# Reordered loads, split key and value weights, and zero products on TensorE at the start of a gated cross-attention and mixture-of-experts kernel

## The chip, the cores and the metric

One NeuronCore of a Trainium2 chip runs the whole program. The metric is the device time in microseconds (us), from a median of three runs. The profile is one execution of the same program; its times are microseconds from the start of its span.

## The reference

```python
x = x + tanh(g_xattn) * xattn(layernorm(x), ctx)   # x: 8 batches x 56 tokens x 256
x = x + tanh(g_ffn)   * moe(layernorm(x))          # 16 experts, 2 per token, one shared

def xattn(x, cond, ...):                           # cond: 8 x 1500 x 256
    q = qdq(x) @ qdq(wq).T + bq                    # qdq: round to int8 and back, by row
    k, v = split(cond @ wkv.T + bkv)               # 256 columns of keys, 256 of values
    attn = softmax(q @ k.T / 4)                    # 16 heads of 16
    return qdq(attn @ v) @ qdq(wp).T + bp
```

Four inputs of this matter here: the tokens x (448 KB), the key and value weights wkv (512 KB), the query weights wq (256 KB) and the context of the first batch, which is loaded in three chunks of 500 context rows (500 KB each).

## The kernel before

Keys and values are computed in 16-bit halves: a high half is a rounded copy, a low half is what the copy lost, and a product is three partial products (high by high, high by low, low by high), each in two parts of 128 for the contraction. So one group of keys (`project_keys(n, u)`) is 6 matmuls of 500 columns, and one group of values (`project_values(n, v)`) is 12 matmuls of 256 columns, all recorded under line 1035 (`split3`). Each batch has 6 groups of each kind. ScalarE (ACT) makes the high halves (`context_hi`, L479; weights L472), VectorE (DVE) the low halves of the first two batches (`context_lo`, L715; weights L721).

There is no planner: each engine has its instructions in an order written out by hand, and waits for counters (semaphores). The order of each engine before the first attention slot, which is what the change touches:

- **SP**, the load queue: tokens (L291), key and value weights in one transfer (L293), context chunk 0, query weights in two transfers (L298), chunks 1 and 2; then the chunks of batch 1, each after the low half of the chunk before it, and the copies that stack the keys (`stack_keys`, L312).
- **ACT**: three small transfers (columns of biases L468, broadcast rows L469, router weights L470), high half of the key and value weights (L472), scaling of the key bias (L565), high halves of chunk 0, tanh of the gate (L567), chunk 1, then keys and values out of the accumulators as TensorE finishes them (`keys_hi` L486, `evacuate_values` L493), between them the query path (L574, L577, L580).
- **DVE**: layer-norm statistics of the tokens (L697 to L703), low half of the weights, low half of chunk 0, `quantise_first` (L708, L678 to L692: the first 112 tokens), low half of chunk 1, low half of the first keys (`keys_lo`, L743), scales (L737), quantisation of the query weights (L678 to L692), low half of chunk 2, second keys, the query product (L749) and its halves, then the other 336 tokens (`quantise_rest`), further keys and the second query product.
- **POOL**: constants (L365 to L385), one power for the layer norm (L390), then more constants, `zero16` among them (L402, 112 x 512 zeros in 16 bits, read only much later).
- **PE** (TensorE): waits for the constants and for the low halves, then keys 0, values 0 and 1, turns the quantised tokens (L1199, L1206), keys 1, turns the query weights (L1223), values 2, first query product (L1213), values 3, keys 2, values 4 and 5, keys 3 and 4, turns the other tokens, keys 5, second query product, and the attention slots (`pe_slot`).

After the prologue come 64 attention slots (8 batches of 8 pairs of heads), in which the keys and values of the next batch are fitted between scores (L1078), turned scores (L1101) and outputs (L1112), then the output projection, the router and the experts.

Of the kernel before, what the change touches and what calls it, by code (L numbers as in the profile page):

```python
# [17 lines left out]
ALU = mybir.AluOpType  # L18
ACT = mybir.ActivationFunctionType
AX = mybir.AxisListType  # L20

B, S, D = 8, 56, 256
# [5 lines left out]
TP, TT = 112, 4  # L28
# [15 lines left out]
NCONST = 24  # L44
NSMALL = 3 * 16
# [64 lines left out]
def program(nc, x, ctx, cols, rows, gate, wq, wkv, wp, W13, W2, out):  # L110
    stack = ExitStack()
    with stack:
# [132 lines left out]
        names = """consts var_ready rstd_ready sp_ready x_loaded wq_loaded wp_loaded wkv_loaded small_loaded xq_ready xr_ready wqq_ready wpq_ready  # L245
# [44 lines left out]
        def _(sp):  # L290
            sp.dma_start(x_in[:], x.rearrange("b s d -> (b s) d").rearrange("(t p) d -> p t d", p=TP)).then_inc(s["x_loaded"], 16)  # L291

            sp.dma_start(wkv_in, wkv).then_inc(s["wkv_loaded"], 16)  # L293
            for c in range(CH):
                sp.dma_start(c_in[:, :, c * CW:(c + 1) * CW], ctx_v[0, :, :, c * CW:(c + 1) * CW]).then_inc(ctx_in[c], 16)
                if c == 0:
                    for k in range(NH):
                        sp.dma_start(wq_in[:, k, :], permuted(wq[k * 128:(k + 1) * 128, :])).then_inc(s["wq_loaded"], 16)  # L298
# [63 lines left out]
        def _(gp):  # L362
            c = Steps(gp, s["consts"])
            for t, v in ((mhalf, -0.5), (unmagic, -MAGIC), (ident, 0.0), (ident16, 0.0), (ones, 1.0), (ones16, 1.0), (before16, 1.0), (hm2, 1.0)):
                c.did(gp.memset(t[:], v))  # L365
# [36 lines left out]
            c.did(gp.memset(zero16[:], 0.0))  # L402
# [28 lines left out]
            gp.wait_ge(s["act_pre"], 3)  # L431
# [33 lines left out]
        def _(act):  # L465
            ap = Steps(act, s["act_pre"])

            act.dma_start(col_in[:], cols).then_inc(s["small_loaded"], 16)  # L468
            act.dma_start(row_in[:], rows.partition_broadcast(TP), allow_slow_non_contiguous=True).then_inc(s["small_loaded"], 16)  # L469
            act.dma_start(gateT[:], gate).then_inc(s["small_loaded"], 16)  # L470
            act.wait_ge(s["wkv_loaded"], 16)
            ap.did(act.activation(wkvT[:, 0], wkv_in, ACT.Copy, scale=WS))  # L472
# [90 lines left out]

            act.wait_ge(s["small_loaded"], NSMALL)
            ap.did(act.activation(bk_c, bk_c, ACT.Copy, scale=WS))  # L565
            context_hi(0, 0)
            ap.did(act.activation(tg[:, 0:1], gx[:, 0:1], ACT.Tanh))  # L567
            context_hi(0, 1)
            act.wait_ge(s["act_pre"], 2)
            keys_hi(0, 0)  # L570
# [4 lines left out]
            evacuate_values(0, 1)  # L575
            act.wait_ge(s["pe_pre"], 2)
            ap.did(act.activation(sx_row[:, 0:TP], PS[:, 1, 0:TP], ACT.Copy))  # L577
            keys_hi(0, 1)
            act.wait_ge(s["pe_pre"], 3)
            ap.did(act.activation(wqT[:], bank16(7)[:, 0:NH * D].rearrange("p (h t) -> p h t", h=NH), ACT.Copy))  # L580
            evacuate_values(0, 2)
# [90 lines left out]
        def _(dve):  # L672
# [44 lines left out]

            dve.wait_ge(s["x_loaded"], 16)
            statistics(x_in, range(TT))
            dve.wait_ge(s["act_pre"], 1)  # L720
            dve.scalar_tensor_tensor(wkvT[:, 1], wkv_in, WS, wkvT[:, 0], ALU.mult, ALU.subtract).then_inc(s["dve_pre"], 1)  # L721
            context_lo(0, 0)
# [16 lines left out]

            def keys_lo(n, u):  # L740
                oh, c = divmod(u, CH)
                need(dve, "kh_done", n * 6 + u + 1)
                dve.scalar_tensor_tensor(KN[:, oh, c, 1, :], PS[:, BANK["K", n, u], 0:CW], bk_c[:, oh:oh + 1],  # L743
                                         KN[:, oh, c, 0, :], ALU.add, ALU.subtract).then_inc(s["kl_done"], 1)
# [19 lines left out]
            context_lo(0, 1)  # L764
            keys_lo(0, 0)
# [6 lines left out]
            dve.wait_ge(s["small_loaded"], NSMALL)  # L772
# [90 lines left out]
            for k, part in enumerate(groups):  # L863
                n = part.stop - part.start
                out_ps = PS[0:TP, out_bank[part.start]:out_bank[part.start] + n, :].rearrange("p t (h j) -> p t h j", j=PW)
                dve.wait_ge(s["pe_post"], k + 1)
                d.did(dve.tensor_scalar(rd[:, part, :], out_ps[:, :, :, DH], WS, None, ALU.mult))
                d.settle()
                d.did(dve.reciprocal(rd[:, part, :], rd[:, part, :]))
                d.settle()  # L870
                dve.tensor_tensor(xn[:, part, :].rearrange("p t (h j) -> p t h j", h=H), out_ps[:, :, :, 0:DH],
                                  rd[:, part, :].unsqueeze(3).to_broadcast([TP, n, H, DH]), ALU.mult).then_inc(s["out_read"], 1)
                dve.wait_ge(s["out_read"], k + 1)
                d.settle()
                d.did(dve.tensor_tensor(xn[:, part, :], xn[:, part, :], bv_r.unsqueeze(1).to_broadcast([TP, n, D]), ALU.add))
                quantise(xn[:, part, :], n, am[0:TP], so[:, part], xq16[:, part, :]).then_inc(s["oq_done"], 1)
# [151 lines left out]
        def _(pe):  # L1028
# [8 lines left out]

            pe.wait_ge(s["consts"], EARLY)
# [150 lines left out]
            project_keys(0, 0)  # L1189
            project_values(0, 0)  # L1190
            project_values(0, 1)

# [25 lines left out]
            project_keys(0, 1)  # L1218
# [218 lines left out]
```

## Time and profile before

| | us |
|---|---|
| device time, median of 3 runs | 407.97 (407.75, 407.97, 412.41) |
| span of the profiled execution | 405.0 |
| PE busy in it | 358.6 |
| DVE busy in it | 303.5 |
| ACT busy in it | 250.9 |
| POOL busy in it | 124.1 |

Of the profiled execution only its span is given, from the first to the last instruction; its device time is not among the numbers shown. The span is 2.97 us under the median of the runs. In the profile, a row of the timeline gives start, duration, engine, line of the code, operation, what is written from what, and the count of instructions merged; the brackets give how long the engine stood idle before it and what ended that.

### The profile page before, as it was taken

How to read it: one execution, taken by the hardware profiler on the slowest of the kernel's cores; microseconds unless marked ns; L12 is line 12 of the kernel's file. 1: busy time of each engine (PE TensorE's matmuls, PEld its weight loads, DVE VectorE, ACT ScalarE, POOL GpSimd, SP SyncE). 2: the span in 40 equal slices, each digit the busy share in tenths (PEclk: the TensorE clock that was granted, in tenths of full speed). 3: DMA queues.
4: the chain of work that ended last, by engine and by line, in shares of the span. 5: the costliest groups of instructions: out<-in, count | busy, mean ns of one | idle time of the engine just before them, and what ended most of it. 6: DMA issues, size and time to landing. Idle time of an engine off the chain costs nothing.

```text
span 405.0 us, 14019 instructions
## 1 busy us (share of the span) xinstructions
PE 358.6 (89%) x5793; PEld 269.3 (67%) x5793; DVE 303.5 (75%) x656; ACT 250.9 (62%) x412; POOL 124.1 (31%) x116
## 2 busy tenths in 40 slices
PE   0896899999998998998999999998864699999993
PEld 0663468668677766855866776786643587888882
DVE  3888886775776676586577668668896877999993
ACT  3476477777686676776768666567721535666761
POOL 6151462132022122222203300001101054787870
PEclk9999699999999999999999999999985858999998
DMA  7869965565294186166336208544000009635001
GB/s 253 196 157 197 241 146 134 87 159 136 58 171 115 53 152 182 54 106 175 103 61 125 54 14 142 129 137 141 3 2 2 1 1 306 191 116 163 2 0 45
DMA packets 34512, 45.65 MB, mean 113 GB/s; under 512 B 3995, under 2 KB 30299, under 8 KB 34323
## 3 DMA queue, kind: packets, MB, share of 16 engines
q1 hardware_dynamic: 33395, 43.74, 44.5%
q0 software_dynamic: 640, 0.78, 0.9%
q8 instruction: 46, 0.75, 0.8%
q10 hardware_dynamic: 416, 0.26, 0.3%
q14 instruction: 15, 0.12, 0.1%
HBM read 25.08 MB, written 0.47 MB: 63 GB/s over the span
## 4 chain that ended last, share of the span: by engine, by line
PE 76%; DVE 13%; issue 5%; ACT 2%; POOL 2%; DMA 1%; DVEq 0%; ACTq 0%; POOLq 0%
PE PS L1035 35%; PE PS L1101 9%; PE PS L1078 8%; PE PS L1112 7%; PE PS L1363 4%; PE PS L1322 3%; DVE mx L794 2%; PE PS L1088 2%; PE PS L1346 2%; PE PS L1312 1%; DMA x_in<-x 1%; DVE KN L743 1%; PE PS L1279 1%; DVE st L697 1%; DVE mtop L798 1%
## 5 line engine op out<-in xcount | busy, mean ns | idle before, releaser
L794 DVE TENSOR_REDUCE mx<-PS 112x1 f32<-112x500 f32 (+1 forms) x128 | 114.3, 933 | 52.8 <-PE PS L1078 52.7
L501 ACT ACTIVATE PT_all<-PS 128x1344 f32<-128x1344 f32 x64 | 82.6, 1290 | 10.1 <-PE PS L1101 9.9
L1035 PE MATMUL PS<-cT,wkvT 128*128 128x500 f16 x288 | 71.5, 385 | 18.0 <-POOL slot_of L404 11.2
L1035 PE MATMUL PS<-wkvT,cT 128*125 128x256 f16 x576 | 73.2, 279 | 0.0
L1035 PEld LDWEIGHTS PS<-wkvT,cT 128*125 128x125 f16 x576 | 65.3, 139 | 5.3 <-issue 0.5
L395 POOL TENSOR_TENSOR cT<-c_in,cT 128x1000 f16<-128x1000 f32 x18 | 37.5, 2082 | 86.9 <-ACT cT L479 86.9
L1035 PEld LDWEIGHTS PS<-cT,wkvT 128*128 128x128 f16 x288 | 27.5, 99 | 50.8 <-POOL slot_of L404 11.2
L486 ACT ACTIVATE KN<-PS,col_in 128x500 f16<-128x500 f32 x48 | 32.5, 677 | 40.6 <-PE PS L1035 40.6
L1078 PE MATMUL PS<-arena,QC 96*112 96x500 f16 x192 | 52.4, 380 | 3.1 <-issue 2.8
L1101 PE MATMUL PS<-QC,arena 98*128 98x112 f16 x768 | 49.2, 214 | 3.0 <-ACT QC L521 2.9
L493 ACT ACTIVATE V<-PS 125x512 f32<-125x512 f32 x48 | 28.7, 598 | 30.6 <-PE PS L1035 30.6
L1101 PEld LDWEIGHTS PS<-QC,arena 98*128 98x128 f16 x768 | 41.6, 99 | 8.3 <-ACT QC L521 3.1
L743 DVE SCALAR_TENSOR_TENSOR KN<-PS,col_in,KN 128x500 f16<-128x500 f32 x48 | 35.2, 736 | 12.8 <-ACT KN L486 12.0
L1112 PE MATMUL PS<-PT_all,V 125*17 125x56 f32 x2592 | 37.8, 213 | 0.1
L449 POOL TENSOR_TENSOR arena<-arena 88x512 f16<-88x512 f32 x17 | 24.8, 1458 | 31.2 <-ACT arena L527 31.1
L1035 PE MATMUL PS<-arena 88*128 88x256 f16 (+2 forms) x216 | 33.3, 306 | 0.8 <-ACT arena L635 0.7
L1112 PEld LDWEIGHTS PS<-PT_all,V 125*17 125x17 f32 x2592 | 33.3, 98 | 0.2 <-issue 0.2
L419 POOL TENSOR_TENSOR QC<-q,par 96x448 f16<-96x448 f16 x16 | 15.0, 943 | 57.1 <-PE PS L1101 55.3
L1035 PEld LDWEIGHTS PS<-arena 88*128 88x128 f16 (+2 forms) x216 | 22.5, 106 | 9.0 <-issue 1.2
L1078 PEld LDWEIGHTS PS<-arena,QC 96*112 96x112 f16 x192 | 20.3, 132 | 9.8 <-issue 3.8
L479 ACT ACTIVATE cT<-c_in 128x1000 f16<-128x1000 f32 x24 | 24.9, 1036 | 2.0 <-DMA c_in<-ctx 1.6
L1088 PEld LDWEIGHTS PS<-ident,nm 112*2 112x2 f16 x64 | 5.1, 79 | 21.9 <-issue 17.3
(207 smaller groups left out, 463.8 us busy)
## 6 DMA issues: line engine op xcount, KB each, us to landing
arena<-KN SPq DMA_DIRECT2D x144, 125.0 KB, 3.6
c_in<-ctx SPq DMA_DIRECT2D x24, 500.0 KB, 4.5
cT<-W SPq DMA_DIRECT2D x11, 352.0 KB
c_in<-W SPq DMA_DIRECT2D x6, 352.0 KB
cT<-W SPq DMA_DIRECT2D x11, 176.0 KB
arena<-place_far SPq DMA_DIRECT2D x1, 1568.0 KB, 10.0
c_in<-W SPq DMA_DIRECT2D x6, 176.0 KB
PT_all<-L_xattn_wkv SPq DMA_DIRECT2D x1, 512.0 KB, 6.1
```

What stands on the lines that cost most here:

```text
L395: gp.tensor_tensor(cT[:, n % 2, 1, :, c * CW:(c + 1) * CW], c_in[:, :, c * CW:(c + 1) * CW], cT[:, n % 2, 0, :, c * CW:(c + 1) * CW], ALU. ...
L449: gp.tensor_tensor(w2T[j % 2][:, 1], w2_s, w2T[j % 2][:, 0], ALU.subtract).then_inc(s["w2l_done"], 1)
L479: act.activation(cT[:, n % 2, 0, :, c * CW:(c + 1) * CW], c_in[:, :, c * CW:(c + 1) * CW], ACT.Copy).then_inc(s["th_done"], 1)
L486: act.activation(KN[:, oh, c, 0, :], PS[:, BANK["K", n, u], 0:CW], ACT.Identity, bias=bk_c[:, oh:oh + 1]).then_inc(s["kh_done"], 1)
L493: act.activation(V[:, n % 2, 2 * v:2 * v + 2, :, 0:DH], PS[0:KP, BANK["V", n, v], :].rearrange("p (t h j) -> p t h j", t=2, h=H), ACT.Copy ...
L501: act.activation(PT_all[:, u % 4, :].rearrange("p (c k) -> p c k", c=CH), PS[:, 3:6, 0:4 * TP], ACT.Exp, scale=SCORE).then_inc(s["exp_done ...
L743: dve.scalar_tensor_tensor(KN[:, oh, c, 1, :], PS[:, BANK["K", n, u], 0:CW], bk_c[:, oh:oh + 1], KN[:, oh, c, 0, :], ALU.add, ALU.subtract ...
L794: dve.tensor_reduce(mx[:, u % 2, k:k + 1], PS[0:TP, k:1 + k * (CH - 1), 0:CW], AX.XY, ALU.max).then_inc(s["red_done"], 1)
L1035: ins = mm(out_, w(a, h), x_(b, h), start=first and k == 0, stop=last and k == len(todo) - 1)
L1078: mm(PS[0:TP, c, 0:CW], QC[0:QR, b % 2, i * TP:(i + 1) * TP], KS[0:QR, b % 2, i, c * CW:(c + 1) * CW], start=True, stop=True).then_inc(s[" ...
L1101: last = mm(PS[:, 3 + t // 4, (t % 4) * TP:(t % 4 + 1) * TP], KS[0:QR + 2, b % 2, i, t * KP:t * KP + 128], QC[0:QR + 2, b % 2, i * TP:(i + ...
L1112: last = mm(PS[32 * j:32 * j + VW, bank, 0:S], V[:, b % 2, t, 4 * hg + j, :], PT[:, (2 * g + j // 2) % 4, t * TP + (j % 2) * S:t * TP + (j ...
```

## The change

The loads go out in the order key weights, chunk 0, value weights, tokens, chunk 1, query weights, chunk 2. The key and value weights come in two transfers with a counter each, and their high and low halves are made apart. ACT issues the broadcast rows and the router weights after the conversion of the key weights; the columns have a counter of their own. `zero16` becomes POOL's first constant, and TensorE multiplies it 24 times into a bank that nothing reads before its next use. On ACT the high half of chunk 1 moves behind the first `keys_hi`; on DVE the statistics move behind the low halves of weights and chunk 0, and `quantise_first` behind the low halves of chunk 1 and of the first keys. On PE keys 1 and values 2 move ahead of the turned tokens, values 3 ahead of the first query product.

```diff
 SP
-  x_in, wkv_in (all), context chunk 0, wq x2, chunk 1, chunk 2
+            sp.dma_start(wkv_in[:, :, 0:D], wkv[:, :, 0:D]).then_inc(s["wk_loaded"], 16)
             for c in range(CH):
                 sp.dma_start(c_in[...c...], ctx_v[0, ...c...]).then_inc(ctx_in[c], 16)
                 if c == 0:
+                    sp.dma_start(wkv_in[:, :, D:2 * D], wkv[:, :, D:2 * D]).then_inc(s["wv_loaded"], 16)
+                    sp.dma_start(x_in[:], ...).then_inc(s["x_loaded"], 16)
+                if c == 1:
                     for k in range(NH): sp.dma_start(wq_in[:, k, :], ...)
 POOL
+            gp.memset(zero16[:], 0.0).then_inc(s["zeros_ready"], 1)
...
-            c.did(gp.memset(zero16[:], 0.0))
 ACT
-            act.wait_ge(s["wkv_loaded"], 16)
-            ap.did(act.activation(wkvT[:, 0], wkv_in, ACT.Copy, scale=WS))
+            act.wait_ge(s["wk_loaded"], 16)
+            ap.did(act.activation(wkvT[:, 0, :, 0:D], wkv_in[:, :, 0:D], ACT.Copy, scale=WS))
...
+            act.dma_start(row_in[:], rows.partition_broadcast(TP), ...)
+            act.dma_start(gateT[:], gate)
             context_hi(0, 0)
+            act.wait_ge(s["wv_loaded"], 16)
+            ap.did(act.activation(wkvT[:, 0, :, D:2 * D], wkv_in[:, :, D:2 * D], ACT.Copy, scale=WS))
+            act.wait_ge(s["col_loaded"], 16)
+            ap.did(act.activation(bk_c, bk_c, ACT.Copy, scale=WS))
+            act.wait_ge(s["act_pre"], 3)
+            keys_hi(0, 0)
+            context_hi(0, 1)
+            act.wait_ge(s["small_loaded"], NSMALL)
+            act.activation(tg[:, 0:1], gx[:, 0:1], ACT.Tanh).then_inc(s["tg_ready"], 1)
             evacuate_values(0, 0)
+            evacuate_values(0, 1)
             context_hi(0, 2)
+            keys_hi(0, 1)
 DVE
+            for k in range(2):
+                part = slice(k * D, (k + 1) * D)
+                dve.wait_ge(s["act_pre"], k + 1)
+                dve.scalar_tensor_tensor(wkvT[:, 1, :, part], wkv_in[:, :, part], WS, wkvT[:, 0, :, part], ...)
+                if k == 0:
+                    context_lo(0, 0)
+            dve.wait_ge(s["x_loaded"], 16)
+            statistics(x_in, range(TT))
+            context_lo(0, 1)
+            keys_lo(0, 0)
             quantise_first()
-            context_lo(0, 1)
-            keys_lo(0, 0)
 PE
+            pe.wait_ge(s["zeros_ready"], 1)
+            for k in range(WARM):            # WARM = 24
+                mm(PS[0:TP, 7, :], zero16[:, 0:TP], zero16[:], start=True, stop=True)
             pe.wait_ge(s["consts"], EARLY)
...
             pe.wait_ge(s["dve_pre"], 1)
             project_keys(0, 0)
+            pe.wait_ge(s["dve_pre"], 2)
             project_values(0, 0)
             project_values(0, 1)
+            project_keys(0, 1)
+            project_values(0, 2)
             turn_tokens([0], 1)
             turn_scales([0], 1)
-            project_keys(0, 1)
             pe.wait_ge(s["wqq_ready"], 1)
...
-            project_values(0, 2)
+            project_values(0, 3)
             pe.wait_ge(s["act_pre"], 6)
             project_queries(...)
-            project_values(0, 3)
```

## Rows read from the trace of the kernel before

**Rows 1.** The page: busy time of each engine; granted TensorE clock in 40 slices.
```profile
PE 358.6 (89%) x5793; PEld 269.3 (67%) x5793; DVE 303.5 (75%) x656; ACT 250.9 (62%) x412; POOL 124.1 (31%) x116
...
PEclk9999699999999999999999999999985858999998
```
**Rows 2.** The page: shares of the chain of work that ended last, by engine.
```profile
PE 76%; DVE 13%; issue 5%; ACT 2%; POOL 2%; DMA 1%; DVEq 0%; ACTq 0%; POOLq 0%
```
**Rows 3.** Timeline, loads landed and converted: start, duration, instruction, [idle before, ended by].
```profile
4.98 1.41 DVE L697 BATCH_NORM_STATS2 st<-x_in 112x6 f32<-112x256 f32 x4 [4.98 <-DMA x_in<-x]
...
7.16 1.04 POOL L390 TENSOR_TENSOR rstd<-var,mhalf 112x4 f32<-112x4 f32 x1 [1.84 <-DVE var L703]
7.36 1.06 ACT L472 ACTIVATE wkvT<-PT_all 128x1024 f16<-128x1024 f32 x1 [3.81 <-DMA PT_all<-L_xattn_wkv]
...
8.45 1.23 DVE L721 SCALAR_TENSOR_TENSOR wkvT<-PT_all,wkvT 128x1024 f16<-128x1024 f32 x1 [1.45 <-ACT wkvT L472]
8.78 1.04 ACT L479 ACTIVATE cT<-c_in 128x1000 f16<-128x1000 f32 x1 [0.27 <-DMA c_in<-ctx]
...
9.85 1.20 DVE L715 TENSOR_TENSOR cT<-c_in,cT 128x1000 f16<-128x1000 f32 x1 [0.18 <-ACT cT L479]
```
**Rows 4.** Timeline, TensorE's first groups and two of the same kind later.
```profile
11.20 2.66 PE L1035 MATMUL PS<-cT,wkvT 128*128 128x500 f16 x6 [11.20 <-POOL slot_of L404]
...
13.65 4.50 PE L1035 MATMUL PS<-wkvT,cT 128*125 128x256 f16 x24
...
23.95 2.78 PE L1035 MATMUL PS<-wkvT,cT 128*125 128x256 f16 x24
...
31.08 1.43 PE L1035 MATMUL PS<-cT,wkvT 128*128 128x500 f16 x6
```
**Rows 5.** Timeline, VectorE from the first tokens to the second query product.
```profile
10.97 0.52 DVE L708 TENSOR_SCALAR xn<-x_in,mv,rstd 112x256 f32<-112x256 f32 x1
...
13.08 0.29 DVE L692 TENSOR_SCALAR xq<-xn 112x256 f16<-112x256 f32 x1
...
14.67 0.74 DVE L743 SCALAR_TENSOR_TENSOR KN<-PS,col_in,KN 128x500 f16<-128x500 f32 x1 [0.19 <-ACT KN L486]
...
17.74 0.43 DVE L692 TENSOR_SCALAR wq<-PT_all 128x512 f16<-128x512 f32 x1
...
20.54 0.74 DVE L743 SCALAR_TENSOR_TENSOR KN<-PS,col_in,KN 128x500 f16<-128x500 f32 x1 [1.26 <-ACT KN L486]
...
21.66 0.58 DVE L749 SCALAR_TENSOR_TENSOR qT<-PS,swq,sx_row 128x112 f32<-128x112 f32 x2 [0.38 <-PE PS L1213]
...
24.86 0.74 DVE L743 SCALAR_TENSOR_TENSOR KN<-PS,col_in,KN 128x500 f16<-128x500 f32 x1 [0.41 <-ACT KN L486]
...
33.19 1.04 DVE L749 SCALAR_TENSOR_TENSOR qT<-PS,swq,sx_row 128x336 f32<-128x336 f32 x2 [0.97 <-PE PS L1213]
```
**Rows 6.** Timeline, ScalarE: high half of chunk 1, and the first keys.
```profile
11.23 1.04 ACT L479 ACTIVATE cT<-c_in 128x1000 f16<-128x1000 f32 x1 [1.31 <-DMA c_in<-ctx]
...
13.96 0.68 ACT L486 ACTIVATE KN<-PS,col_in 128x500 f16<-128x500 f32 x1 [1.70 <-PE PS L1035]
```
**Rows 7.** Timeline: the zeros, and one of ACT's transfers being issued.
```profile
1.25 0.51 ACTq L469 DMA_DIRECT2D row_in<-rows  x1
...
10.26 0.63 POOL L402 MEMSET zero<- 112x512 f16 x1
```
**Rows 8.** DMA view of 0 to 40 us: GB/s in each microsecond; one load's size and landing.
```profile
GB/s 0 20 119 371 327 274 253 369 379 395 404 185 118 122 172 148 300 306 191 83 92 352 297 162 36 59 191 208 71 14 237 134 174 135 142 142 156 156 299 411
...
PT_all<-L_xattn_wkv SPq DMA_DIRECT2D x1, 512.0 KB, 6.1
```
**Rows 9.** Later: TensorE's longest early gap, then busy times and granted clock (PEclk).
```profile
40.84 2.50 PE L1035 MATMUL PS<-cT,wkvT 128*128 128x500 f16 x6 [2.35 <-DVE cT L715]
...
40.00:45.00 5.00, 3.20 (x14) 1.33 (x14) 3.86 (x8) 1.57 (x3) 0.00 (x0) 0.61 1.04 276
45.00:50.00 5.00, 5.00 (x30) 3.02 (x28) 4.12 (x6) 2.63 (x4) 4.01 (x6) 0.71 1.13 206
```

More of the change, by code:

```diff
@@ L43 @@
 EARLY = 16
-NCONST = 24
-NSMALL = 3 * 16
+NCONST = 23
+NSMALL = 2 * 16
+WARM = 24
 ROWS = 2 * D + E + 2
@@ L466, in _ @@
             ap = Steps(act, s["act_pre"])
-            act.dma_start(col_in[:], cols).then_inc(s["small_loaded"], 16)
-            act.dma_start(row_in[:], rows.partition_broadcast(TP), allow_slow_non_contiguous=True).then_inc(s["small_loaded"], 16)
-            act.dma_start(gateT[:], gate).then_inc(s["small_loaded"], 16)
-            act.wait_ge(s["wkv_loaded"], 16)
-            ap.did(act.activation(wkvT[:, 0], wkv_in, ACT.Copy, scale=WS))
+            act.dma_start(col_in[:], cols).then_inc(s["col_loaded"], 16)
+            act.wait_ge(s["wk_loaded"], 16)
+            ap.did(act.activation(wkvT[:, 0, :, 0:D], wkv_in[:, :, 0:D], ACT.Copy, scale=WS))
             def context_hi(n, c):
@@ L562, in act_slot @@
                     w13_hi(0)
-            act.wait_ge(s["small_loaded"], NSMALL)
[L565 to L570, printed above, removed]
+            act.dma_start(row_in[:], rows.partition_broadcast(TP), allow_slow_non_contiguous=True).then_inc(s["small_loaded"], 16)
+            act.dma_start(gateT[:], gate).then_inc(s["small_loaded"], 16)
+            context_hi(0, 0)
+            act.wait_ge(s["wv_loaded"], 16)
[5 more added lines that the diff above has]
+            context_hi(0, 1)
+            act.wait_ge(s["small_loaded"], NSMALL)
+            act.activation(tg[:, 0:1], gx[:, 0:1], ACT.Tanh).then_inc(s["tg_ready"], 1)
             evacuate_values(0, 0)
+            evacuate_values(0, 1)
             context_hi(0, 2)
+            keys_hi(0, 1)
             act.wait_ge(s["pe_pre"], 1)
             ap.did(act.activation(xqT[:, :, 0:TP], bank16(7)[:, 0:NH * TP].rearrange("p (h t) -> p h t", h=NH), ACT.Copy))
-            evacuate_values(0, 1)
             act.wait_ge(s["pe_pre"], 2)
             ap.did(act.activation(sx_row[:, 0:TP], PS[:, 1, 0:TP], ACT.Copy))
-            keys_hi(0, 1)
+            evacuate_values(0, 2)
             act.wait_ge(s["pe_pre"], 3)
             ap.did(act.activation(wqT[:], bank16(7)[:, 0:NH * D].rearrange("p (h t) -> p h t", h=NH), ACT.Copy))
-            evacuate_values(0, 2)
             context_hi(1, 0)
@@ L716, in context_lo, with keys_lo @@
                                   cT[:, n % 2, 0, :, c * CW:(c + 1) * CW], ALU.subtract).then_inc(s["tl0_done"], 1)
+            def keys_lo(n, u):
+                oh, c = divmod(u, CH)
+                need(dve, "kh_done", n * 6 + u + 1)
+                dve.scalar_tensor_tensor(KN[:, oh, c, 1, :], PS[:, BANK["K", n, u], 0:CW], bk_c[:, oh:oh + 1],
+                                         KN[:, oh, c, 0, :], ALU.add, ALU.subtract).then_inc(s["kl_done"], 1)
+            for k in range(2):
+                part = slice(k * D, (k + 1) * D)
+                dve.wait_ge(s["act_pre"], k + 1)
+                dve.scalar_tensor_tensor(wkvT[:, 1, :, part], wkv_in[:, :, part], WS, wkvT[:, 0, :, part],
+                                         ALU.mult, ALU.subtract).then_inc(s["dve_pre"], 1)
+                if k == 0:
+                    context_lo(0, 0)
             dve.wait_ge(s["x_loaded"], 16)
             statistics(x_in, range(TT))
-            dve.wait_ge(s["act_pre"], 1)
-            dve.scalar_tensor_tensor(wkvT[:, 1], wkv_in, WS, wkvT[:, 0], ALU.mult, ALU.subtract).then_inc(s["dve_pre"], 1)
-            context_lo(0, 0)
+            context_lo(0, 1)
+            keys_lo(0, 0)
             def quantise_first():
```

15 lines of the change are left out of this document (5 added, 10 removed).

## The prediction

> **What bounds the kernel now.** I read the busy shares first: PE is busy for 89% of the span, DVE for 75% [rows 1]. The chain of waits agrees: 76% of the span is PE work, 13% DVE [rows 2]. The change touches none of that bulk. It can only move the moment at which the attention slots begin, and every microsecond gained there is one at the end, since the slots follow at PE's pace. So the timeline of the first 35 us decides, with one question: which engine sets that moment?
>
> There, PE stands idle until 11.20 us. It waits for the low half of chunk 0, which DVE ends at 9.85 + 1.20 = 11.05; the profile names POOL's L404, but that is only the last event by time, and PE waits for nothing POOL does then [rows 3, 4]. Before it the loads land one behind the other: tokens at 4.96, weights at 7.35, chunk 0 at about 8.75 [rows 3]. PE's first groups take long besides: six 500-column matmuls start 2.45 us before the next group, 0.408 each, and later ones take 1.43 for six with their tail. The 24 value matmuls take 4.50 against 2.78 [rows 4]. So the first matmuls are at the 1.2 GHz level, the later at 2.4.
>
> But PE catches up, and what then holds the slots is DVE. From 8.45 on it is almost never idle: its waits before the second query product are 0.19, 1.26, 0.38, 0.41 and 0.97 [rows 5]. That product starts at 33.19 and ends at 34.23; the first scores wait for it. A change that starts PE sooner is worth only what it takes out of those waits, or what it moves DVE's work forward.
>
> **Loads.** I add up the GB/s row: 0.51 MB are moved by 4 us, 0.84 by 5, 1.11 by 6, 1.36 by 7, 1.73 by 8, 2.11 by 9, 2.51 by 10 [rows 8]. The combined weights land at 1.25 + 6.1 = 7.35, when 1.49 MB are through; ahead of their end stand 0.98 MB of SP loads and 0.25 of ACT's. So a load lands when the curve passes its bytes plus some 0.27. Key weights (0.26 MB): about 4.1. Chunk 0 (0.77): 5.8, or 6.7 if ACT's 0.25 MB, issued by then, get their share in front; I take 6.0. Value weights: 7.5. Tokens: 8.7. Chunk 1: 10.1. Query weights 10.8.
>
> **ACT and DVE up to chunk 0.** Half of the 1.06 conversion, with its fixed part, is about 0.6 [rows 3]: ACT has the key weights by 4.75, DVE by 5.4. ACT then issues two transfers, 0.51 for such a one [rows 7], until 5.8, hidden by the wait for chunk 0. Chunk 0 is high at 7.1 and low at 8.3. That is 2.75 us sooner than 11.05. The halves cost one more fixed part on each engine, about 0.1, in waits.
>
> **Zero products.** POOL's zeros take 0.63 [rows 7] from 0.8, so PE starts at 1.45; POOL's other constants slip by as much and nobody waits for them. 24 products of 512 columns take 0.418 each at the lower clock (0.408 x 512/500) and 0.215 at the higher (0.21 for 500, from 1.43 less a tail of 0.17). The bounds are 1.45 + 5.2 = 6.6, all at the higher, and 1.45 + 10.0 = 11.5, all at the lower. How long was the clock low before? With x us at 0.209 per value matmul and the rest at 0.108, 24 = x/0.209 + (4.33 - x)/0.108 gives x = 3.6: low from 11.20 to 17.25, 6.0 us [rows 4]. I take that row: 14.4 products at 0.418, 9.6 at 0.215, and the end at **9.55**. That is 1.25 after the data at 8.3: the zero products, not the loads, now start the first keys, still 1.65 sooner than 11.20.
>
> **Where the gain goes.** Keys 0 are ready at 9.55 + 1.43 = 11.0, against 13.86. ACT now has the high half of chunk 1 behind `keys_hi` of that group: 0.68 from 11.05, then 1.04 [rows 6], so chunk 1 is high at **12.8**; before it was at 11.23 + 1.04 = 12.27, with PE's results not in its way. DVE has by then done value weights and statistics (from 8.3: 0.6, tokens at 8.7, statistics from 4.98 to 7.0 before, so 2.05; end at 11.0) and waits 1.8 us. POOL's power of 1.04 [rows 3] falls into that wait, nothing. Queued behind the wait are low half 1.2, keys and scales and query weights 3.50 (from 14.67 to 17.74 + 0.43), first tokens 2.40 (10.97 to 13.37) [rows 5]: 7.1 in all, so the query weights are quantised at **19.95**. Before: 18.17. DVE is 1.8 late, because it lost its free start: statistics were done while it waited for weights.
>
> Then it gains. Chunk 2 low 1.2 and keys 1 0.74 follow without the 1.26 wait, since PE has keys 1 at 15.3; they end at 21.95. PE turns the query weights at 20.0 (0.22), does values 3 (1.30) and the product (0.2) by 21.9. So the first query product starts at about 22.0 against 21.66, 0.35 late; the 0.41 wait of the third keys goes too, which leaves -0.05. The last wait, 0.97, stays: it hangs on DVE's own quantisation through ACT, PE, keys 5 and the product, and the change shortens none of it. The moved SP loads: query weights at 10.8 are needed at 17, chunk 2 at 13.6 or later, the copies of keys before the slots. The rows land near 11 to 12, needed by the tanh at 12.8. Sum: **-0.1 us, 407.9** on the median, or 404.9 on the profiled span; the 2.97 between the two is left as it is.
>
> **The rivals.** *Early rise* (0.25). If the clock rises earlier after the zeros begin, data at 8.3 starts the keys: 1.25 sooner than 9.55, and each step above hangs on that start, so 406.7. With ten products at the lower clock or fewer this holds nearly in full. For it: the length of 6.0 is one sample. Against: that one sample. The Trainium skill (TensorE: Matmul & The Clock Gate, Part 1: The HAM clock gate) says that the number of cold matmuls at a start varies from run to run, 6, 11 or 14 for one kernel; with 6 the products would end near 7.8 and the result would be this rival's. The trace at 14.4 agrees only with the top of it.
>
> *Clock lost in a new gap* (0.22, slower). PE has nothing between its scales at 17.7 and the query weights at 19.95, 2.25 us, after a gap of 0.6. In the trace a gap of 2.35 was followed by 2.50 for six matmuls instead of 1.43, and by a granted clock of 0.61 and 0.71 in the next ten us [rows 9]. Then turned weights, values 3 and the product take 3.44 instead of 1.72: 23.55 instead of 22.0, +1.55, and the third keys add 0.3: 409.8. A second gap, 28.3 to 30.3, would cost the 3.1 of PE work in the last link instead: 411. Below 2 us of gap, with the clock kept, it costs nothing. Against: the gap of the trace is one gap, and the longer of the two.
>
> *The zeros do not raise the clock* (0.06). They end at 11.5, 1.95 later than forecast, and the first real groups are at the lower clock as well: about 410.5. *Order of arrival* (0.05): tokens landing after 10.7 instead of 8.7 delay statistics past chunk 1, microsecond for microsecond: 409. *The late dip goes* (0.05, on top of the first): in the ten us from 40 PE is busy for some 6.0 us at half clock [rows 9], worth up to 3.0; a start shifted by a us may spare it: 404. The forecast has the remaining 0.37.
>
> **Numbers.** Predicted 407.9. The range 405.4 to 410.3 holds the forecast, the early rise, the gap rival but for its second half, and leaves about 2 in 10; the forecast's own range, with the zeros ending 0.6 sooner or later, is 407.2 to 408.6. Two per cent is 8.2 us, about what a measurement of this kernel can tell from no change. No case here reaches it: gains end at about 4 us and losses at 3 to 5. Within 2%: 0.95; faster by more: 0.02; slower by more: 0.03 (two lost clocks and one late load).
>
> **What would show it.** PE's zeros end at 9 to 10 and the first keys start there; ACT's L479 for chunk 1 starts right behind its first L486; DVE is idle for 1 to 2 us ahead of its second L715; the query weights are done at 19.5 to 20.5; second query product near 33.1. The early rise shows as keys at 8.3 and this product near 32. The lost clock shows as 0.4 us matmuls after 20. I am wrong if DVE's chain is not what holds the slots, so that the first scores move with PE.

## The result, and the profile after

The changed kernel takes **418.67 us** (median of 4 runs, 416.23 to 421.5), beside 410.19 (407.75 to 412.42) for the kernel before on the same chip. The ratio is 1.0211, 95% interval 1.0133 to 1.0288: slower beyond the noise, though the interval leaves open whether by two per cent. Forecast were 407.9 and a range of 405.4 to 410.3; the time lies above it, and to "slower by more than two per cent" I had given 0.03. The profiled executions are 419.8 us of span after and 405.0 before, so 14.8 us are to be explained there, more than the 8.5 between the medians: the execution that was profiled after the change is the slowest of its four (421.5). Medians in this document are over all runs of a kernel, while the ratios leave out the executions in a second, slower state of the chip, and so does the table below, which for that reason lacks e8.

The page after. The q8 row is the queue that carries instructions; before, it had 46 packets and 0.75 MB.

```profile
PE 370.1 (88%) x5817; PEld 275.6 (66%) x5817; DVE 306.1 (73%) x657; ACT 251.5 (60%) x413; POOL 124.2 (30%) x116
...
PEclk9989878998998999999999999899995578999998
...
q8 instruction: 47, 0.77, 0.8%
...
PE 73%; DVE 13%; issue 6%; ACT 4%; DMA 2%; SPq 1%; POOL 0%; DVEq 0%; ACTq 0%
```

PE is busy 11.5 us longer than in [rows 1] with 24 more matmuls, and "issue" has grown from 5% to 6% of a longer chain [rows 2]. Six of the first twenty slices of the granted clock are below 9, before one.

The prologue of the changed kernel, from its timeline (start, duration, instruction, [idle before, ended by]):

```profile
1.38 8.28 PE L1050 MATMUL PS<-zero 112*112 112x512 f16 x24 [1.38 <-POOL zero L366]
9.50 1.43 PE L1045 MATMUL PS<-cT,wkvT 128*128 128x500 f16 x6
...
11.03 0.68 ACT L486 ACTIVATE KN<-PS,col_in 128x500 f16<-128x500 f32 x1 [2.31 <-PE PS L1045]
11.96 1.04 ACT L479 ACTIVATE cT<-c_in 128x1000 f16<-128x1000 f32 x1 [0.26 <-DMA c_in<-ctx]
13.03 1.20 DVE L720 TENSOR_TENSOR cT<-c_in,cT 128x1000 f16<-128x1000 f32 x1 [1.02 <-ACT cT L479]
...
19.91 0.43 DVE L697 TENSOR_SCALAR wq<-PT_all 128x512 f16<-128x512 f32 x1
20.40 0.40 PE L1238 MATMUL PS<-ident,wq 128*128 128x128 f16 x4 [2.10 <-DVE wq L697]
20.63 2.49 PE L1045 MATMUL PS<-wkvT,cT 128*125 128x256 f16 x12
...
34.06 1.04 DVE L760 SCALAR_TENSOR_TENSOR qT<-PS,swq,sx_row 128x336 f32<-128x336 f32 x2 [0.89 <-PE PS L1229]
...
35.32 0.81 PE L1091 MATMUL PS<-arena,QC 96*112 96x500 f16 x3 [1.36 <-issue]
```

The first keys start at 9.50 (before 11.20), the query weights are done at 20.34, and the second query product starts at 34.06 against 33.19 [rows 5]. The first scores came at 34.44 before. So the first scores come 0.9 us later, and the other 14 us arose behind them, where the change edits nothing.

**Where they arose.** Each of the 64 slots has one ACT operation for its exponentials (L501, `PT_all<-PS`). I read its start in the timelines and subtract. These are single profiled executions; "pairs" is the number of zero products added at TensorE's start (each a matmul and a weight load), and e1 to e12 are the experiments below.

```
          pairs  1st    5th    25th   64th   | 1st to 5th  5th to 64th
before      0   45.80  63.85 146.24 293.76 |   18.05       229.91
after      24   46.48  69.77 159.93 308.98 |   23.29       239.21
e2          0   43.12  66.40 148.63 296.50 |   23.28       230.10
e7          0   44.04  64.50 146.11 294.81 |   20.46       230.31
e1         24   44.21  67.49 157.50 307.76 |   23.28       240.27
e3         24   43.34  66.63 156.90 301.90 |   23.29       235.27
e4         24   43.38  63.84 152.84 297.85 |   20.46       234.01
e6         64   44.95  68.15 148.47 290.95 |   23.20       222.80
e9         64   45.82  67.67 147.99 290.48 |   21.85       222.81
e10     24+40   45.77  63.82 144.13 286.57 |   18.05       222.75
e5        128   46.59  68.36 149.72 297.80 |   21.77       229.44
e11        64   43.52  59.56 141.28 284.85 |   16.04       225.29
e12        64   45.63  61.60 143.53 288.44 |   15.97       226.84
```

After against before: +0.68 at the first, +5.24 from there to the fifth, +9.30 from the fifth to the last, and -0.4 behind it (419.8 - 308.98 against 405.0 - 293.76). Sum 14.8.

**The 9.3: TensorE waits for instructions.** Timeline of the changed kernel, TensorE, in two slots of that stretch, then busy times and granted clock (PEclk) around the first of them, then the instruction queue in the half microsecond from 93.0:

```profile
92.36 1.37 PE L1125 MATMUL PS<-PT_all,V 125*17 125x56 f32 x95
95.79 0.22 PE L1125 MATMUL PS<-PT_all,V 125*17 125x56 f32 x1 [2.06 <-issue]
...
133.02 0.28 PE L1125 MATMUL PS<-PT_all,V 125*17 125x56 f32 x3 [2.34 <-issue]
```
```profile
90.00:95.00 5.00, 3.73 (x116) 2.42 (x113) 3.01 (x6) 3.82 (x5) 0.44 (x1) 1.00 0.66 186
95.00:100.00 5.00, 4.21 (x22) 2.39 (x22) 2.11 (x4) 1.51 (x2) 1.64 (x1) 0.66 0.54 157
```
```profile
q8 instruction: 1, 0.02, 12.8%
```

The outputs of a slot are 96 pairs issued in 1.2 us. After 95 of them TensorE stands still for 2.06 us with nothing to wait for ("issue"), and then does the 96th. A packet of 16 KB (0.77 MB over 47) starts on the instruction queue 2.4 us ahead of the restart. In the next row the granted clock is 0.66 instead of 1.00: part of its matmuls run at the 1.2 GHz level. The kernel after has seven idle stretches of 0.5 us or more between 60 and 285 us (six marked "issue", one put down to POOL), 10.3 us in all, and three clock losses there; before has five (four and one), 5.4 in all, and no clock loss. Each of the three takes 1.7 us of full clock, here (1.00 - 0.66) x 5 us. So an estimate of the stretch's loss is 5.0 us of halts and 5.1 of clock, 10.1 in all, beside the 9.3 measured.

That these halts belong to the boundaries of pieces can be counted. I put TensorE's records (weight loads, matmuls and waits) in order of their start, in the traces of the kernels before and after and of e1 to e12. Between 60 and 285 us they have 58 idle stretches of 0.5 us or more, and in 57 of them the number of records ahead of the restart leaves 193 to 196 when divided by 256, whatever the kernel and whatever wait the profile names. In each of the 57 a 16 KB packet had started 2.25 to 3.57 us before the restart. The Trainium skill (Advanced Engine Details and Errata, ISA Cache) gives a line of that memory as 16 KB, 256 instructions; the traces agree by this count. The Trainium skill (Runtime: NRT & Kernel Launch, Instruction fetch mechanics) calls the crossing of such a boundary mostly hidden; here 25 of 32 in this stretch of the changed kernel are, also 18 of the 20 that lie in outputs, and the two others there cost 2.06 and 2.34 us. What differs is when the next packet starts: 2.2 to 5.0 us behind the boundary before it at the seven halts, 0.3 to 1.4 at 18 of the other 25. Why it starts late there is not known.

**The 5.2: VectorE is shut out by POOL.** The timeline of the changed kernel, and behind it that of the kernel before:

```profile
52.16 1.82 POOL L421 TENSOR_TENSOR QC<-q,par 96x448 f16<-96x448 f16 x2
52.45 5.63 DVE L807 TENSOR_TENSOR mtop<-mx 112x1 f32<-112x1 f32 x1
53.95 4.11 POOL L398 TENSOR_TENSOR cT<-c_in,cT 128x1000 f16<-128x1000 f32 x2
...
59.26 2.66 PE L1045 MATMUL PS<-cT,wkvT 128*128 128x500 f16 x6 [4.32 <-DVE KN L726]
```
```profile
52.89 2.09 POOL L395 TENSOR_TENSOR cT<-c_in,cT 128x1000 f16<-128x1000 f32 x1
53.53 1.47 DVE L798 TENSOR_TENSOR mtop<-mx 112x1 f32<-112x1 f32 x1
...
55.51 2.08 POOL L395 TENSOR_TENSOR cT<-c_in,cT 128x1000 f16<-128x1000 f32 x1 [0.53 <-ACT cT L479]
```

The maximum of two numbers per partition takes 5.63 us, until 58.08, just when POOL's four tensor operations in a row end at 58.06. Before, it met only one of them and took 1.47, ending as that one ends (54.98). The Trainium skill (SBUF — State Buffer, on the two separate sides) says that POOL and a VectorE operation with two SBUF inputs share a port pair as an exclusive lock held for the whole instruction; the trace agrees. Here VectorE did not get through between POOL operations that follow without a gap. That is not always so: in the kernel before, an operation of 2.20 us (L803, from 48.96) ends at 51.16, as POOL's L436 does (51.14), although POOL's next one runs on from 51.10. What decides it is open. PE stands 4.32 us behind the 5.63 and restarts at the lower clock. Which of these meetings occur depends on shifts of a microsecond between the engines.

### The profile page after: what moved, and what is told of

Read it like the earlier page. It is cut to its first block, busy times and chain, and to the rows that moved or that the text cites. A ratio compares the mean times of both kernels' runs of the same rounds, so it can differ in the third digit from the quotient of the medians.

```text
span 419.8 us, 14071 instructions
## 1 busy us (share of the span) xinstructions
PE 370.1 (88%) x5817; PEld 275.6 (66%) x5817; DVE 306.1 (73%) x657; ACT 251.5 (60%) x413; POOL 124.2 (30%) x116
## 4 chain that ended last, share of the span: by engine, by line
PE 73%; DVE 13%; issue 6%; ACT 4%; DMA 2%; SPq 1%; POOL 0%; DVEq 0%; ACTq 0%
PE PS L1045 34%; PE PS L1114 10%; PE PS L1091 8%; PE PS L1125 7%; PE PS L1377 4%; PE PS L1336 3%; DMA c_in<-ctx 2%; PE PS L1101 2%; DVE mtop L807 1%; PE PS L1360 1%; DVE mx L803 1%; DVE KN L726 1%; DVE cT L720 1%; DVE am L683 1%; PE PS L1293 1%
## 5 line engine op out<-in xcount | busy, mean ns | idle before, releaser
L803 DVE TENSOR_REDUCE mx<-PS 112x1 f32<-112x500 f32 (+1 forms) x128 | 114.4, 934 | 63.0 <-PE PS L1091 62.8
L501 ACT ACTIVATE PT_all<-PS 128x1344 f32<-128x1344 f32 x64 | 82.6, 1290 | 12.0 <-PE PS L1114 11.9
L1045 PE MATMUL PS<-cT,wkvT 128*128 128x500 f16 x288 | 73.0, 391 | 10.9 <-DVE KN L726 4.3
L1045 PE MATMUL PS<-wkvT,cT 128*125 128x256 f16 x576 | 75.1, 282 | 2.4 <-issue 1.3
L1045 PEld LDWEIGHTS PS<-wkvT,cT 128*125 128x125 f16 x576 | 66.5, 141 | 7.9 <-issue 2.8
L1045 PEld LDWEIGHTS PS<-cT,wkvT 128*128 128x128 f16 x288 | 28.3, 101 | 43.5 <-issue 12.8
L1114 PE MATMUL PS<-QC,arena 98*128 98x112 f16 x768 | 50.3, 217 | 3.4 <-ACT QC L521 3.3
L1114 PEld LDWEIGHTS PS<-QC,arena 98*128 98x128 f16 x768 | 42.6, 100 | 8.9 <-ACT QC L521 3.6
L726 DVE SCALAR_TENSOR_TENSOR KN<-PS,col_in,KN 128x500 f16<-128x500 f32 x48 | 35.3, 736 | 13.5 <-ACT KN L486 12.8
L1091 PEld LDWEIGHTS PS<-arena,QC 96*112 96x112 f16 x192 | 20.6, 134 | 7.9 <-issue 2.1
L1101 PEld LDWEIGHTS PS<-ident,nm 112*2 112x2 f16 x64 | 5.1, 79 | 23.3 <-issue 16.4
```

The source lines that it names most:

```text
L501: act.activation(PT_all[:, u % 4, :].rearrange("p (c k) -> p c k", c=CH), PS[:, 3:6, 0:4 * TP], ACT.Exp, scale=SCORE).then_inc(s["exp_done ...
L803: dve.tensor_reduce(mx[:, u % 2, k:k + 1], PS[0:TP, k:1 + k * (CH - 1), 0:CW], AX.XY, ALU.max).then_inc(s["red_done"], 1)
L1045: ins = mm(out_, w(a, h), x_(b, h), start=first and k == 0, stop=last and k == len(todo) - 1)
L1091: mm(PS[0:TP, c, 0:CW], QC[0:QR, b % 2, i * TP:(i + 1) * TP], KS[0:QR, b % 2, i, c * CW:(c + 1) * CW], start=True, stop=True).then_inc(s[" ...
L1114: last = mm(PS[:, 3 + t // 4, (t % 4) * TP:(t % 4 + 1) * TP], KS[0:QR + 2, b % 2, i, t * KP:t * KP + 128], QC[0:QR + 2, b % 2, i * TP:(i + ...
```

## The experiments

All compute the whole reference. Ratios are to the kernel before on the same chip.

**e1: the kernel before with 24 pairs of 2 columns, hidden in TensorE's first wait.** Nothing else of the change, except that `zero16` becomes POOL's first constant, as there.

```
+            gp.memset(zero16[:], 0.0).then_inc(s["zeros_ready"], 1)
...
+            pe.wait_ge(s["zeros_ready"], 1)
+            for k in range(24):
+                mm(PS[0:TP, 7, 0:2], zero16[:, 0:TP], zero16[:, 0:2], start=True, stop=True)
             pe.wait_ge(s["consts"], EARLY)
```

> The kernel before with 24 products of two columns of zeros at TensorE's start, in the time in which it waits for data anyway: nothing is reordered, only TensorE's instruction stream is longer by 48 instructions ahead of all work (24 matmuls, 24 weight loads), and the zeros are written first on POOL. Instruction-fetch theory (TensorE's stream arrives in 16 KB pieces, and where a piece ends in a dense stretch of the slots TensorE stands still until the next has come): the stalls of 0.5 to 2.4 us once a batch move into other work and grow as in the kernel after, from 6 us in sum to about 9 to 10, with one to four more stretches at the lower clock; 3 to 8 us slower than the kernel before. Port theory (POOL's work back to back holds VectorE's small operations for 5.6 us once, at 52 us): no such stall here, time as before within 1.5 us.

Measured: 423.15 (419.12 to 427.48), ratio 1.0311, 95% 1.021 to 1.0413. 48 tiny instructions, over long before data arrives, cost the old kernel as much as the whole change or more (the intervals overlap), and more than the 3 to 8 us expected. The first scores are even early, at 33.05. From its timeline:

```profile
94.01 0.25 PE L1116 MATMUL PS<-PT_all,V 125*17 125x56 f32 x1 [2.62 <-issue]
...
132.26 0.28 PE L1116 MATMUL PS<-PT_all,V 125*17 125x56 f32 x3 [2.06 <-issue]
```

The same halts in the same slots: after 95 pairs in one, ahead of the last 3 in the other. A third of 2.06 us follows at 167.50. The shut-out of VectorE, which I had expected to be absent, is there too (5.64 us from 50.18). The order of loads and the split weights are not in this kernel, so they are not needed for the loss.

**e2: the change without the zero products** (their two lines and the wait deleted).

> The kernel after without its 24 zero products and the wait for the zeros; order of loads and work as in the kernel after. Instruction-fetch theory: the pieces of TensorE's stream end about where they did before, the stalls of the slots are those of the kernel before (sum about 6 us), and 3 to 8 us of the loss are gone. Port theory: the stall of VectorE near 52 us depends on how TensorE's slots stand to POOL's work there; with TensorE colder it is likely gone too, so its presence or absence in the trace decides, worth 4.3 us plus 1.7 of lower clock. If the loss is in the order of the prologue alone, this kernel is as slow as the kernel after.

Measured: 411.18 (407.7 to 414.46), ratio 1.0047, 95% 0.9999 to 1.0095. Nearly all of the loss went with the 24 products; e3 tells their number from their length. From the fifth slot to the last it needs 230.10 us, the kernel before 229.91. The shut-out of VectorE stays (5.62 us), and eats what the start had gained: first scores at 33.21.

**e3: the change with its 24 products cut to 2 columns** (`0:2` as in e1).

> The kernel after with each of its 24 zero products cut from 512 to 2 columns: same number of instructions, next to no time and no raising of the clock. Instruction-fetch theory: against the same kernel without zero products it is slower by 3 to 8 us, with the stalls where the kernel after has them, in values and outputs once a batch. Theory that the products' time or the clock matters: equal to the kernel without them.

Measured: 415.36 (414.32 to 415.85), ratio 1.015, 95% 1.0082 to 1.0218. Same count, almost none of the TensorE time: most of the loss stays (the interval overlaps that of the changed kernel), with halts of 2.33 and 2.34 in the same two slots. Here the query weights gave the same idle 2.10 as in the changed kernel, but the clock stayed up:

```profile
19.69 0.40 PE L1238 MATMUL PS<-ident,wq 128*128 128x128 f16 x4 [2.10 <-DVE wq L697]
19.92 1.48 PE L1045 MATMUL PS<-wkvT,cT 128*125 128x256 f16 x12
```

Twelve value matmuls took 1.48 us, not the 2.49 of the changed kernel. A gap of 2.10 loses the clock or keeps it.

**e4: the change, with POOL's two token operations (0.62 + 2.35 us) moved behind batch 2's low halves**, to take POOL's queue of work out of VectorE's way. **e7** is the same without the zero products, **e8** the same edit in the kernel before.

```
-            gp.tensor_tensor(bp_r, bp_r, tg[:, 0:1].to_broadcast([TP, D]), ALU.mult)...
-            gp.tensor_tensor(x1[:], x_in[:], bp_r.unsqueeze(1).to_broadcast([TP, TT, D]), ALU.add)...
             for b in range(B - 1):
...
+                if b == 0:
+                    (the same two, with their waits)
```

> The kernel after with POOL's two operations on the token residual (0.62 and 2.35 us, before batch 1's queries) moved behind POOL's low halves of batch 2. Port theory: POOL reaches batch 1's queries and the first low halves 3 us sooner, a gap opens between its operations, and VectorE's 112x1 operation that took 5.63 us at 52.45 takes 0.2 to 1.5; the wait of 4.3 us of TensorE behind it and one stretch at the lower clock go: 4 to 6 us faster than the kernel after. Instruction-fetch theory alone: no change beyond 1.5 us.

> The kernel after without zero products and with POOL's two operations on the token residual moved behind the low halves of batch 2. Fetch and port theories together: alignment as in the kernel before, and the collision near 50 us smaller or gone (5.62 us for a 112x1 operation in the kernel without zero products). 1 to 5 us faster than the kernel without zero products (411.2), so 406 to 410, about level with or better than the kernel before. If the collision only moves to another small operation of VectorE, the gain is 1.5 or less.

> The kernel before with POOL's two operations on the token residual moved behind the low halves of batch 2. In the kernel before two small VectorE operations took 2.20 and 1.47 us beside POOL's work. Port theory: by the pattern, either both shrink (1 to 3 us faster), or POOL's queries and first low half now run back to back against the maxima of an earlier slot (a stall of 4 us, up to 3 us slower). Fetch theory: no effect.

Measured: e4 415.31 (410.86 to 416.77), ratio 1.0134, 1.0046 to 1.0222; e7 410.18 (405.03 to 413.43), 0.9979, 0.9936 to 1.0023; e8 408.94 (403.78 to 417.13), 0.9967, 0.9922 to 1.0012. A miss: neither e7 nor e8 differs from the kernel before by more than its interval, and e4 lies 0.8 points below the changed kernel, some 3 us where 4 to 6 were expected, with overlapping intervals and both halts in the outputs still there (2.33 and 2.62 us). The timeline of e4 shows why:

```profile
45.66 4.27 DVE L813 SCALAR_TENSOR_TENSOR nm<-mtop,nm 112x1 f16<-112x1 f32 x1
46.03 1.83 POOL L421 TENSOR_TENSOR QC<-q,par 96x448 f16<-96x448 f16 x2
47.82 2.08 POOL L398 TENSOR_TENSOR cT<-c_in,cT 128x1000 f16<-128x1000 f32 x1
```

The collision has only moved to another two-input operation, of an earlier slot, and costs 4.27 instead of 5.63, ending as POOL's third operation does (49.90). It starts 0.37 us ahead of the first of them, while POOL is still issuing transfers (L431, until 46.01). Reordering POOL's work shifts the shut-out; it does not remove it.

**e5 and e6: as e1, with 128 pairs and with 64.** 128 pairs are 256 instructions, one whole piece; 64 are half a piece. This tells the fetch from its rival, that a longer stream simply costs more.

> The kernel before with 128 two-column products of zeros at TensorE's start: 256 instructions more, one whole 16 KB piece of its stream, some 8 to 12 us long at about 0.1 us each in the earlier run, so they end near the time the data lands (11.2 us) or up to 3 us behind it. Instruction-fetch theory by alignment: the pieces end where they do in the kernel before, the stalls are those of the kernel before (sum about 6 us, none of 2 us in the outputs), and the time is that of the kernel before plus what the products delay the start, 0 to 3 us. Rival, any longer stream costs: at least as slow as with 24 such products, 12 to 17 us over the kernel before.

> The kernel before with 64 two-column products of zeros: half a piece (128 instructions). Instruction-fetch theory by alignment: another pattern of stalls than with 0, 24 or 128; where a piece ends moves by half a piece, so that stalls of 2 us in the outputs may come in other batches or be gone; anywhere from 2 us faster to 12 us slower, with the sum of TensorE's unexplained stalls in the trace going with it. Rival, any longer stream costs: between the runs with 24 and 128.

Measured: e5 412.36 (408.71 to 414.65), ratio 1.007, 1.0026 to 1.0113; e6 **405.61** (401.84 to 407.44), ratio 0.9884, 0.981 to 0.9959. So 0, 24, 64 and 128 pairs give ratios of 1, 1.031, 0.988 and 1.007. The longer-stream rival falls: the time goes up, down and back. With one whole piece the stretch from the fifth slot to the last is as before (229.44 to 229.91). What e5 has more, 4.1 us of span, lies ahead of it: 0.8 at the first exponentials, where the zeros hold the first keys to 13.35, and 3.7 from there to the fifth, with a shut-out of 5.62 us that the kernel before does not have. With half a piece the pattern is another one. The outputs from 60 to 285 us, of e6 and then of the changed kernel (busy, mean ns | idle before):

```profile
L1116 PE MATMUL PS<-PT_all,V 125*17 125x56 f32 x2496 | 36.1, 213 | 0.0
```
```profile
L1125 PE MATMUL PS<-PT_all,V 125*17 125x56 f32 x2421 | 35.6, 213 | 4.4 <-issue 4.4
```

TensorE never stands for 0.5 us in these 225 us of e6, although 20 of its 35 boundaries lie in outputs. Its shut-out of VectorE is there in full (5.63 us at 50.92), so the two losses are independent.

**e9: the change with 64 short products** instead of 24 long ones.

> The kernel after with 64 two-column zero products in place of its 24 long ones: its order of loads and work, TensorE's stream moved by half a 16 KB piece, as in the best run so far on the order of the kernel before. Fetch theory: no stall of over 0.5 us between slots 1 and 60 but the collision near 50 us, so 10 to 15 us faster than the kernel after (418.7) and within 2 of 405.6, a little under it if the new order is worth its 0.5 to 1 us. If the new order itself loses time, 408 or more.

Measured: 403.87 (402.41 to 405.3), ratio 0.9866, 0.9817 to 0.9915. No halts again, 222.81 us from the fifth slot to the last. By the ratios, which is how runs on different chips compare, the rest of the change is worth 0.2% against e6 (0.9866 to 0.9884), with intervals that overlap: about nothing, as forecast.

**e10: the change whole, its long products kept, and 40 short pairs more** in TensorE's wait for the query weights, so that the pieces stand behind it as in e9.

```
             turn_scales([0], 1)
+            for k in range(40):
+                mm(PS[0:TP, 3, 0:2], zero16[:, 0:TP], zero16[:, 0:2], start=True, stop=True)
             pe.wait_ge(s["wqq_ready"], 1)
```

> The kernel after, unchanged but for 40 two-column zero products into a free bank, in the 2.1 us in which TensorE waits for the query weights: they cost up to 1.7 us there, and move everything behind them to the same half-piece alignment. Fetch theory: every part of the change is still in it, yet 8 to 14 us faster than the kernel after. Rival, the zero products or the order lose the time: at or above 418.7.

Measured: **403.28** (399.93 to 405.01), ratio 0.985, 0.9794 to 0.9907. Adding 80 instructions to the changed kernel takes it from a ratio of 1.0211 to 0.985, more than the 8 to 14 us expected. The windows of 60 to 285 us, for after, before and e10 in this order (us, busy PE, PEld, DVE, ACT, POOL, PEclk, DMA share, GB/s):

```profile
60.00:285.00 225.00, 214.66 (x3951) 159.00 (x3953) 147.40 (x301) 148.01 (x221) 44.34 (x28) 0.97 0.46 103
```
```profile
60.00:285.00 225.00, 217.56 (x4284) 161.24 (x4285) 157.81 (x327) 156.95 (x234) 45.82 (x29) 1.00 0.50 112
```
```profile
60.00:285.00 225.00, 222.13 (x4437) 165.64 (x4436) 164.64 (x341) 162.96 (x244) 47.01 (x30) 1.00 0.51 112
```

In the same 225 us the kernel after gets through 3951 matmuls, before 4284, e10 4437. The 40 products themselves lie in the gap, and the clock falls after them all the same:

```profile
17.48 2.18 PE L1235 MATMUL PS<-zero 112*112 112x2 f16 x40
...
19.97 2.14 PE L1045 MATMUL PS<-wkvT,cT 128*125 128x256 f16 x12
```

e10 also had no long shut-out (2.20 and 1.46 us, as before), which is 5.2 us of its gain in the profile (18.05 against 23.29): nothing in the edit aims at it.

**e11 and e12: e6 and e9 with the maxima rewritten so that no VectorE operation of theirs has two SBUF tensors as inputs.**

```
-  tensor_tensor(mtop, mx[..0], mx[..1], max)
+  tensor_reduce(mtop, mx[..0:2], max)
   tensor_scalar(nm16[..0], mtop, -1/CS, mult)
-  scalar_tensor_tensor(nm16[..1], mtop, -1/CS, nm16[..0], mult, subtract)
+  tensor_scalar(nm32, nm16[..0], 1.0, mult)
+  tensor_scalar(nm16[..1], mtop, -1/CS, nm32 (one value per partition), mult, subtract)
```

> The kernel before with 64 two-column zero products, and with the maxima's small VectorE operations rewritten to read one tensor each (a reduction for the maximum of two, a 32-bit copy of the high half used as a per-partition scalar for the low half): one operation of 0.16 more in each of the 64 slots. Port theory, that only an operation with two tensors in SBUF waits for POOL: no small operation over 1 us near 50, the 4.3 us wait of TensorE and one stretch at the lower clock gone, 3 to 5 us faster than 405.6 less what the longer chain costs, 0 to 2. Rival, any VectorE operation waits for POOL there: the same stall under another line, and 0 to 2 us slower than 405.6.

> Both of these in the order of the kernel after: 64 short products and maxima that read one tensor each. If fetch alignment and the port are the two causes and the new order is neutral or worth up to 1 us, this is the best, 399 to 404, faster than both kernels.

Measured: e11 **400.85** (398.32 to 402.97), ratio 0.9795, 0.9736 to 0.9854; e12 401.86 (397.81 to 403.43), ratio 0.9804, 0.9746 to 0.9861. e11's timeline in the place of the collision:

```profile
49.38 1.82 POOL L421 TENSOR_TENSOR QC<-q,par 96x448 f16<-96x448 f16 x2
49.49 0.15 DVE L800 TENSOR_REDUCE mtop<-mx 112x1 f32<-112x2 f32 x1
...
51.16 4.12 POOL L398 TENSOR_TENSOR cT<-c_in,cT 128x1000 f16<-128x1000 f32 x2
...
53.98 0.22 DVE L807 TENSOR_SCALAR nm<-mtop,nm 112x1 f16<-112x1 f32 x1
```

POOL runs as long as before, and VectorE's small operations pass it in 0.15 to 0.22 us. From the first slot to the fifth both kernels take 16.0 us, where the others take 18.05 to 23.3. Part is given back: the stretch to the 64th slot is 2.5 (e11) and 4.0 us (e12) longer than in e6 and e9, and four waits of 0.7 to 1.3 us are back in it, three of them at a boundary of pieces. One more VectorE operation now stands between scores and exponentials; that it is the cause is a guess. e11 and e12 have the lowest times of this case: 2% below the kernel before, and 4% below the changed one by the two ratios. Their intervals overlap those of e9 and e10, and e11's that of e6, so that the shut-out is gone is shown by the trace, and what it is worth in time is not settled.

## Why the prediction was wrong

**The step that failed** is the first one: "The change touches none of that bulk. It can only move the moment at which the attention slots begin, and every microsecond gained there is one at the end". The bulk's instructions are the same, but the change touches it in two ways. It puts 48 instructions in front of TensorE's stream, which moves every boundary between 16 KB pieces by 48: 9.3 us (after against before from the fifth slot to the last), shown by e1, e2, e6 and e10. And it shifts the engines against each other by about a microsecond, which turned shut-outs of 1.5 to 2.2 us into one of 5.63: 5.2 us. That the two-input operations are the cause is shown by e11. Different shifts bring it about: e1, e5 and e6 (zeros alone) and e2 (all but the zeros) have it too. But e10, with all of the change and 40 pairs more, has only the short ones of the kernel before. I had the price of 24 products in columns and clock, and none for their being instructions. My own top line, "No case here reaches" two per cent, rested on the same step.

**The steps of the prologue held, but for the loads.** Zero products end at 9.5 and the first keys start at 9.50 (forecast 9.55): the 14.4 cold products were nearly right. Chunk 1's high half was to be ready at 12.8 and was at 13.00, though for another reason than given: ACT waited for the load, which landed at about 11.95 and not at 10.1. VectorE waited 1.02 ahead of the second low half (forecast 1.8, its statistics ending later). Query weights: 19.95 forecast, 20.34 measured. The landings were read off the curve of the kernel before, as if the new order would move bytes as fast. It did not: by 10 us 2.16 MB were through, not 2.51. In the DMA view of 0 to 40 us of the changed kernel, GB/s in each microsecond:

```profile
GB/s 0 2 109 310 366 284 282 258 254 290 234 304 365 378 120 104 248 167 112 231 57 50 63 238 377 164 93 217 203 112 13 216 164 160 144 141 139 155 160 276
```

The start came out 1.0 above the sum of -0.1, by the late landings and a rival.

**Clock lost in a new gap** (0.22): its mechanism came true in the changed kernel, with a gap of 2.10 and matmuls at the 1.2 GHz level from about 20.6. Its price can be read against e4, which has the same orders on all engines but POOL, the same zeros and the same gap, and kept the clock: its query weights were done 0.67 sooner (19.67) and its first scores came 1.83 sooner (33.49). That leaves an estimate of 1.2 us for the clock, where I had put 1.9. Single traces scatter about as much: the first scores come at 33.05 to 34.44 with the old orders (e5 aside, whose zeros are in the way) and at 33.21 to 35.91 with the new ones, so no trace shows that the new orders start the slots sooner. Which of the two happens is not fixed by the length of the gap: e3 and e4 kept the clock after the same 2.10, and e10 lost some of it with the gap filled by 2-column products. **Early rise** did not happen: the zeros held the first keys until 9.35 to 9.69 in the three kernels that have the long ones. **Zeros that do not raise the clock** is refuted: six key matmuls took 1.43 at 9.50. In e3, with 2-column products, the same six took 2.66, as in [rows 4], and so they did in e5, where such products run up to them without a gap. So the long products do raise the clock; that brings nothing that shows at the end: e9, without long products, takes 403.87, and e10, with them, 403.28. **Order of arrival**: tokens landed at 9.98, later than 8.7 and sooner than the 10.7 of that rival; chunk 1 was the later one. In e9, with the same loads, the statistics began at 11.76 and the first scores at 35.91, so this rival was real. **The late dip**: in [rows 9] the clock was 0.61 and 0.71 from 40 to 50; after had 0.66 from 40 to 45 and 0.50 from 60 to 65, so it was not spared.

"Every microsecond gained there is one at the end" failed in the other direction too: e2 brought the first scores forward by 1.2 us (33.21) and ended no sooner than the kernel before, because VectorE was then shut out for longer.

**Still open.** Only four offsets were tried, so 64 is the best of four and not the best. With 24 pairs the stretch from the fifth slot to the last ranges from 234.0 to 240.3 in four kernels; the place of a boundary can be counted, but not what it costs: that goes with how late the next packet starts, and what delays it no run here shows. Nor is it known why e11 and e12 lose 2.5 to 4.0 us in the later slots.

## What to carry to other kernels

Adding or removing instructions on TensorE anywhere moves all piece boundaries behind them: before crediting or blaming an edit for a change of one to three per cent, look for idle stretches of 0.5 to 2.6 us with no work to wait for, most of them marked "issue", whose places in TensorE's stream differ by multiples of 256 instructions, and repeat the comparison with the same count of instructions (pad with short products in a wait). Here it also paid in the trace to keep two-input VectorE operations out of a critical chain while POOL works on tensors, however small they are; a reduce or an operation with a per-partition value does the same and passed (0.15 to 0.22 us). And when an edit shifts engines that were tuned against each other, forecast a range as wide as the collisions that the trace already shows, not only the sum of the steps.

## What the hardware showed that I had not expected

- TensorE halts of 2.06 to 2.62 us where a piece of instructions ends inside 96 pairs of tiny float32 matmuls and the next 16 KB packet starts late; 57 of 58 idle stretches of 0.5 us or more lie at the same place of 256 instructions. 24 pairs more at the start cost 3.1%, 64 gain 1.2%, 128 cost 0.7%.
- A 112x1 VectorE operation held for 5.63 us behind four POOL operations in a row; the median of its 64 executions is 0.16.
- Zero products of 2 columns cost about 0.1 us each at the start (64 in 6.13 us) and 0.05 later (40 in 2.18), and do not raise the clock: the six key matmuls behind them still took 2.66 us, also in e5, where no gap lies between.
